# Attention and mixture-of-experts kernel: order of the work in the first and the last expert step

## What is computed

```python
x = x + attention(layernorm(x), ctx_1024, mask)
flat = layernorm(x).reshape(T, 256)
probs = softmax(flat @ router_w)                  # 8 experts
topk_w, topk_idx = top_k(probs, 2)
topk_w = topk_w / clip(topk_w.sum(-1), 1e-9)
h = silu(einsum('td,edf->etf', flat, w1[e]))      # 256 -> 512
y = einsum('etf,efd->etd', h, w2[e])              # 512 -> 256
out = x + sum over the two chosen experts of topk_w * y
```

## Time and profile before

| | us |
|---|---|
| median of three runs | 481.57 |
| lowest and highest | 479.81, 481.71 |
| the profiled execution | 480.16 |
| its span in the profile | 478.4 |
| PE busy | 422.5 |
| DVE busy | 347.5 |
| ACT busy | 268.6 |
| POOL busy | 189.4 |
| PE's mean granted clock | 0.946 |

### The profile page before, as it was taken

The page is one execution under the profiler, slowest core; times in us unless marked ns, Lnnn a source line. Parts: engine busy times, 40 slices in busy tenths (PEclk is TensorE's granted clock), DMA queues, the critical chain, the costliest instruction groups (busy, mean ns, idle before and its releaser), DMA issues.

```text
span 478.4 us, 10876 instructions
## 1 busy us (share of the span) xinstructions
PE 422.5 (88%) x4215; PEld 381.9 (80%) x4215; DVE 347.5 (73%) x775; ACT 268.6 (56%) x356; POOL 189.4 (40%) x158
## 2 busy tenths in 40 slices
PE   2877999999999999999999986778999999999720
PEld 2666788889888888988878985768999999999610
DVE  4886777778777777777776877747777777777454
ACT  3762656665666666566565871037666777766200
POOL 7614333222444322342100000073777877876410
PEclk9987999999999999999999999589999999999865
DMA  8999976778887777976410260364787777775168
GB/s 197 244 267 286 274 202 147 149 150 189 179 186 153 179 166 164 194 177 136 97 38 26 90 219 1 103 246 129 261 262 256 260 254 249 247 247 187 57 196 287
DMA packets 75123, 87.90 MB, mean 184 GB/s; under 512 B 20240, under 2 KB 66992, under 8 KB 75072
## 3 DMA queue, kind: packets, MB, share of 16 engines
q1 hardware_dynamic: 69136, 74.36, 60.0%
q0 software_dynamic: 4032, 11.02, 6.4%
q10 hardware_dynamic: 1904, 1.84, 1.1%
HBM read 51.23 MB, written 16.90 MB: 142 GB/s over the span
## 4 chain that ended last, share of the span: by engine, by line
PE 77%; DVE 6%; DMA 5%; issue 3%; SPq 3%; ACT 2%; POOL 1%; POOLq 0%; DVEq 0%
PE ps L1455 33%; PE ps L1515 11%; PE ps L1544 9%; PE ps L1530 9%; PE ps L1478 6%; PE ps L1650 2%; PE ps L1774 2%; DMA mask_scratch<-mask_rows 1%; PE ps L1557 1%; DVE neg_max L1014 1%; DMA upper_y<-y_rows 1%; DMA rows<-xn_rows,token_of_row 1%; DMA y_rows<-y_out,y_row_of_row 1%; POOL rows L681 1%; DMA q_stack<-q_lo 1%
## 5 line engine op out<-in xcount | busy, mean ns | idle before, releaser
L1014 DVE TENSOR_REDUCE neg_max<-ps 112x1 f32<-112x376 f32 x256 | 132.4, 545 | 37.9 <-PE ps L1515 34.0
L747 ACT ACTIVATE probs<-ps 125x1344 f32<-125x1344 f32 x64 | 82.8, 1293 | 51.3 <-PE ps L1530 50.4
L1515 PE MATMUL ps<-k_stack,q_stack 98*112 98x376 f32 x256 | 82.7, 365 | 4.6 <-DVE neg_max L1014 2.4
L587 POOL TENSOR_TENSOR k_lo<-k_f,k_hi 128x752 fp32r<-128x752 f32 x16 | 28.8, 1803 | 143.9 <-ACT k_hi L721 133.5
L689 POOL DMA_INDIRECT y_rows<-y_out,y_row_of_row x42 | 63.4, 1511 | 31.7 <-DVE y_out L1352 20.4
L681 POOL DMA_INDIRECT rows<-xn_rows,token_of_row x42 | 42.8, 1019 | 44.2 <-DVE y_row_of_row L1306 31.7
L1515 PEld LDWEIGHTS ps<-k_stack,q_stack 98*112 98x112 f32 x256 | 42.0, 177 | 17.1 <-DVE neg_max L1014 10.8
L1455 PE MATMUL ps<-w_hi,h_hi 128*128 128x256 f32 x168 | 49.8, 297 | 5.0 <-issue 3.4
L1530 PE MATMUL ps<-q_stack,k_stack 100*125 100x224 f32 x384 | 53.9, 276 | 0.3 <-ACT probs L747 0.3
L1530 PEld LDWEIGHTS ps<-q_stack,k_stack 100*125 100x125 f32 x384 | 49.6, 188 | 1.7 <-ACT probs L747 1.2
L1455 PE MATMUL ps<-flat_t_hi,w_hi 128*128 128x256 f32 x168 | 47.4, 282 | 2.8 <-DVE flat_t_lo L1334 2.8
(11 more groups left out here) (197 smaller groups left out, 982.6 us busy)
## 6 DMA issues: line engine op xcount, KB each, us to landing
w_raw<-w SPq DMA_DIRECT2D x42, 512.0 KB, 4.3
k_stack<-k_hi SPq DMA_DIRECT2D x64, 188.0 KB, 4.8
k_stack<-k_lo SPq DMA_DIRECT2D x32, 188.0 KB, 5.5
ctx_raw<-ctx_t SPq DMA_DIRECT2D x32, 187.5 KB, 2.8
q_stack<-q_scratch SPq DMA_DIRECT2D x30, 168.0 KB
q_scratch<-q_hi SPq DMA_DIRECT2D x16, 224.0 KB, 3.7
xn_rows<-xn SPq DMA_DIRECT2D x14, 256.0 KB, 2.5
keep<-keep_scratch SPq DMA_DIRECT2D x14, 188.0 KB, 3.8
```

Source lines behind the costliest of these rows:

```text
L587: pool.tensor_tensor(kl[:, :, :], kf[:, :, :], kh[:, :, :].bitcast(F32), ALU.subtract)\
L747: act.activation(pf[j % 2][:, :, :], ps[0:CT, BK_ST:BK_ST + KT, 0:4 * S], ACT.Exp).then_inc(pf_ready, 1)
L1014: dve.tensor_reduce(neg_max[:, s:s + 1], ps[0:S, BK_MAX + s % 2, 0:CP], AX.X, ALU.max, negate=True).then_inc(max_read, 1)
L1515: pe.matmul(ps[0:S, BK_MAX + a, 0:CP], qs[b.ring][0:R_MAX, q, S * a:S * (a + 1)], ks[b.ring][0:R_MAX, q, :], start=True, stop=True).then_i ...
```

## The change

Only the code of ACT and DVE changes, and there only the first step (0) and the last (20).

```diff
@@ scalar engine
+            def load_silu_table():
+                act.activation(eps_c[:, :], eps_c[:, :], ACT.Silu)
+
+            def first_step(t):
+                w1_high(t.after(1))
+                w2_high(t)
+                rows_high(t.after(1))
+                silu(t)
+
+            def last_step(t):
+                w2_high(t)
+                silu(t)
...
-            for n in range(-1, STEPS):
+            zeroth = Batch(0, 0)
+            w1_high(zeroth)
+            load_silu_table()
+            rows_high(zeroth)
+            first_step(zeroth)
+            for n in range(1, STEPS - 1):
                 step(Batch(0, n))
+            last_step(Batch(0, STEPS - 1))
@@ vector engine
+            def first_expert_step(t):
+                after = t.after(1)
+                split_low(after, w_raw[after.par][0], w1h, w1l, w1h_ready, w1l_ready)
+                split_low(t, w_raw[t.par][1], w2h, w2l, w2h_ready, w2l_ready)
+                rows_low(after)
+                h_low(t)
+
+            def last_expert_step(t):
+                split_low(t, w_raw[t.par][1], w2h, w2l, w2h_ready, w2l_ready)
+                h_low(t)
+                y_rows_out(t.after(-1))
...
-            for n in range(-1, STEPS + 1):
+            expert_step(Batch(0, -1))
+            first_expert_step(Batch(0, 0))
+            for n in range(1, STEPS - 1):
                 expert_step(Batch(0, n))
+            last_expert_step(Batch(0, STEPS - 1))
+            y_rows_out(Batch(0, STEPS - 1))
```

## The result

| | before | changed |
|---|---|---|
| median | 481.25 us (479.81 to 481.71, 4 runs) | 473.78 us (472.46 to 474.64, 4 runs) |
| ratio to before | | 0.9849, 95% interval 0.9817 to 0.988 |
| profiled execution, its span | 480.16, 478.4 | 473.56, 471.8 |
| PE's mean granted clock | 0.946 | 0.956 |

The changed kernel is 1.5% faster: 7.5 us between the medians, 6.6 between the two spans. The forecast was 474.9 us, the range 472.5 to 478.0.

The account below looks back on a forecast made before the run. The prediction took TensorE to bound the middle steps, with winnable holes at both ends. Gains of 1.7 (start) and 4.2 (end) sum to 5.9 us: 474.3 from the profile, 475.7 from the median; forecast 474.9, range 472.5 to 478.0.

Parts of the forecast that it names:

- The start: Step 0: table load and second weights leave the path behind step 1's rows, PE becomes next to be late; gain 1.7 us.
- The end up to the last product: Step 20: no PE hole, clock stays 1.00, product 3.0 us instead of 5.5; last output copies start 5.6 us earlier.
- The scatters and the lower reads: Tail: step 19's scatters take 0.97 us each, `lower_y` reads start 0.73 us earlier; step 20's second scatter lands after 4.91.
- The overlap of the two groups of reads: Tail: `upper_y` reads meet `lower_y` reads on the DMA engines and lose 1.5 us, leaving the end 4.2 us gain.
- a second way gives the same: Tail check: DMA engine times 6.8 and 11.5 us back to back from 454.3, plus 1.6, also end at 474.2.
- the overlap free: Rival, tail: reads and output writes keep their old pattern, everything behind the last product moves by 5.7 us; 472.8 us; chance 0.1.
- the sum from the median: Whole kernel: the same 5.9 us gain taken from the 481.57 us median instead of the profiled execution gives 475.7 us.
- The last scatter late: Rival, tail: the last scatter lands only after 7.4 us, with seven reads queued; gain 1.7 + 3.2, 475.3 us; chance 0.12.
- the last weights late: Rival, last step: step 20's second weights land after about 444.1, delaying silu; with 3 us late, about 478 us; chance 0.05.
- the DVE loop: Rival, middle steps: scatters against DVE instructions make DVE the one to wait; 19 steps lose up to 14 us, 488; chance 0.03.

Follow-up runs that it names:

- changed_again: The changed kernel measured once more, with no further edit, beside later experiments: 474.62 us, ratio 0.988 to before.
- halves_out: Changed kernel, plus the last product's first 128 rows signalled separately and its second half in another PSUM bank: 472.62 us, ratio 0.9842 to before.
- end_only: Changed kernel with its first step put back to the old order, without the early table load: 476.01 us, ratio 0.9901 to before.

## Why the prediction was right, and where it was short

**The start, 1.7 us.** Right: 1.6 by five profiles with A of 5.5 us. The 0.1 is a slip of reading: PE's hole of 1.74 us came from adding the chain's 0.44 us to a start from the order in time (324.90), where the row says 0.60; PE was free at 325.50, and the hole was 1.58 us. The table load cost nothing in its new place, the second weights neither, and what is late next is PE. In the profiled execution itself 0.6 us of it was lost to ACT's late start on step 1's rows.

**The end up to the last product.** Right in each link. Step 20's second weights were there in time: ACT waited for them until 442.99, counted from step 19's copies 4.86 us ahead (forecast: 443.4 with copies at 448.45, 5.05 ahead):

```profile
442.99 1.05 ACT L911 CAST w_hi<-w_raw 128x1024 fp32r<-128x1024 f32 x1 [1.10 <-DMA w_raw<-w]
```

That left 0.46 us until silu at 444.50 (0.7 forecast). `h_lo` ended with PE's last matmul of step 19, the clock stayed at 1.00, the product took 3.07 us (3.0 forecast). Last copies relative to step 19's: 5.55 us earlier, 5.6 forecast.

**The scatters and the lower reads.** Right: 0.97 us for step 19's first scatter, lower reads 0.72 us earlier from the copies (0.73 forecast). Step 20's second scatter landed 4.67 us after issue (4.91 taken).

**The overlap of the two groups of reads** is the term that was mis-sized: +1.5 us in the forecast, -0.2 measured (13.9 from the upper reads to the end, 14.1 before). I had treated the DMA engines' busy time (6.8 and 11.5 us) as a fixed price of these bytes, and a share of 0.96 as full. It is neither: the bytes took 16.3 us in the changed kernel, and the trace of before has single microseconds, one under the lower reads and one under the output writes, that were there to be read beside the 0.96:

```profile
456.00:457.00 1.00, 1.00 (x5) 0.73 (x4) 0.00 (x0) 0.00 (x0) 0.00 (x0) 0.50 1.16 350
474.00:475.00 1.00, 0.00 (x0) 0.00 (x0) 0.34 (x1) 0.00 (x0) 0.00 (x0) 0.50 1.10 386
```

A group alone leaves rate unused although the share reads 0.96. The check "a second way gives the same" was no check, since it rested on the same assumption. So the rival that I gave 0.1, the overlap free, is what happened; its 472.8 us and the forecast's 474.9 lie on either side of the 473.78 measured. That 474.9 came within 1.1 us is in part luck: the sum from the median gave 475.7, 1.9 too high, and 474.9 was a choice between it and 474.3.

**The last scatter late, the last weights late, the DVE loop:** none occurred in the profile of the changed kernel. The last scatter landed within 4.0 to 5.9 us in the ten profiles whose upper reads waited for it, never 7.4. The weights came closer than the 0.05 suggests: in changed_again the cast began 4.42 us ahead of the copies (445.52) and silu followed it with nothing in hand (446.57 to 446.59), so a load later by more would have cost time. The loop over DVE ran at the same pace: from step 0's second product to step 19's it took 118.45 us in the changed kernel (326.30 to 444.75), 118.37 before (327.08 to 445.45).

**By the sum:** 5.9 us forecast; 6.6 between the profiles, with 0.6 lost at the start, so 7.2 without that loss, beside the 7.4 of free overlap; 7.5 between the medians.

## What to carry to other kernels

In a pipeline whose middle is bound by one engine, look at the first and last iteration by themselves: the order that is free in the middle puts work on the path at the ends, where the other engines have nothing else to hide it behind. A hole ahead of the last product was paid three times here, as idle time, as half the clock behind it, and as a gap in the reads that follow. And do not add up DMA groups by their busy share: queue the second group early and measure what the two take together, since earlier still need not be better (halves_out: 1.1 us earlier, 0.2 to 0.6 won).

## What the runs showed of the hardware that was not expected

- Seven reads of 256 KB by themselves moved 281 to 290 GB/s at a share of 0.87 to 0.94 of the 16 DMA engines; with seven more queued behind them, 328 to 334 GB/s at 1.00 to 1.03. Single microseconds reached a share of 1.16.
- The granted clock behind a hole of PE of the same 3.16 us was 0.50 for the whole product in two executions and 0.65 and 0.68 on average in two others; a hole of 1.98 us gave 0.63 once, one of 1.58 us left it at 1.00.
- A low granted clock was also seen in the first products of the expert steps in two of twelve profiles (0.50 over 5.45 us, 0.65 over 4.5 us), behind waits of 0.7 to 1.4 us that in other profiles left it at 1.00. It cost 2.5 and 1.5 us there, once with the new start (changed_again) and once with the old (end_only).
